# Moving the first units of cross attention into the heads of the last causal batch

## The reference

```
q = x@Wq; c = x@Wkv_down; k = c@Wk_up; v = c@Wv_up      (16 heads of 32, rotary on 24 of 32)
x = layernorm(x + causal_softmax(q k^T / sqrt(32)) v)
s = coef * (x @ W_qkv[:D].T) @ ctx^T                      (ctx: 4 x 512 x 512, keys and values)
keep the 54 largest scores of a row, softmax over them
x = layernorm(x + (att @ ctx) @ W_o.T)
x = layernorm(x + mixture of 8 gated experts(x), weights from a router)
```

## Time and profile before

| | us |
|---|---|
| median of 3 runs (1635.18 to 1636.54) | 1636.16 |
| the profiled execution | 1635.91 |
| its span, first to last instruction | 1634.1 |
| PE busy in it | 1471.2 (90%) |
| DVE busy | 1186.5 (73%) |
| ACT busy | 900.4 (55%) |
| POOL busy | 767.7 (47%) |

### The profile page before, as it was taken

The page is one execution under the profiler, slowest core; times in us unless marked ns, Lnnn a source line. Parts: engine busy times, 40 slices in busy tenths (PEclk is TensorE's granted clock), DMA queues, the critical chain, the costliest instruction groups (busy, mean ns, idle before and its releaser), DMA issues.

```text
span 1634.1 us, 27867 instructions
## 1 busy us (share of the span) xinstructions
PE 1471.2 (90%) x10404; PEld 902.3 (55%) x10404; DVE 1186.5 (73%) x2030; ACT 900.4 (55%) x1452; POOL 767.7 (47%) x693
## 2 busy tenths in 40 slices
PE   6898888988788898587999999999999999999984
PEld 3466666566544454243665666566656665666554
DVE  4767787968459999967776667666766676667657
ACT  4367575766544553555465556555655565556542
POOL 5355362712212314888474456445644564456422
PEclk9799988988599999788999999999999999999997
DMA  9500010002011110210010001000110011000002
GB/s 288 213 27 2 29 53 29 27 28 104 27 52 52 52 53 1 65 66 13 27 40 26 27 26 36 31 27 27 35 32 27 26 29 37 27 27 28 12 1 103
DMA packets 68173, 74.72 MB, mean 46 GB/s; under 512 B 9021, under 2 KB 46525, under 8 KB 67017
## 3 DMA queue, kind: packets, MB, share of 16 engines
q1 hardware_dynamic: 67464, 68.73, 13.0%
q10 hardware_dynamic: 576, 4.19, 0.7%
HBM read 49.66 MB, written 10.49 MB: 37 GB/s over the span
## 4 chain that ended last, share of the span: by engine, by line
PE 65%; DVE 13%; issue 8%; POOL 6%; ACT 4%; DVEq 0%; ACTq 0%; POOLq 0%
PE banks L1177 48%; PE banks L920 6%; PE banks L1029 2%; PE banks L1013 2%; DVE nmf L1566 2%; PE banks L974 2%; PE banks L991 1%; POOL xsum L824 1%; POOL xsum L821 1%; ACT pf L1271 1%; DVE top L1698 1%; DVE wk L1694 1%; PE banks L1015 1%; DVE attf L1705 1%; POOL xc L829 1%
## 5 line engine op out<-in xcount | busy, mean ns | idle before, releaser
L1177 PE MATMUL banks<-xc,w 128*128 128x512 f16 x2688 | 588.7, 381 | 15.8 <-ACT banks L1220 15.8
L1177 PEld LDWEIGHTS banks<-xc,w 128*128 128x128 f16 x2688 | 263.7, 98 | 335.4 <-ACT banks L1220 21.2
L1177 PE MATMUL banks<-wd,mid 128*128 128x256 f16 x2688 | 296.5, 273 | 4.7 <-ACT banks L1220 2.8
L1177 PEld LDWEIGHTS banks<-wd,mid 128*128 128x128 f16 x2688 | 262.8, 98 | 39.3 <-ACT banks L1220 3.1
L897 POOL TENSOR_TENSOR mid<-m,mid 128x512 f16<-128x512 f32 x64 | 75.0, 1172 | 315.0 <-ACT mid L1220 314.9
L1220 ACT ACTIVATE banks<-banks 128x512 f32<-128x512 f32 x192 | 108.3, 578 | 186.5 <-PE banks L1177 186.5
L897 POOL TENSOR_TENSOR mid<-msum,mid 128x512 f16<-128x512 f32 x128 | 185.8, 1470 | 1.3 <-ACT mid L1220 1.3
L1511 DVE SCALAR_TENSOR_TENSOR w<-stage,w 128x512 f16<-128x512 f32 (+1 forms) x56 | 62.2, 1150 | 104.4 <-ACT w L1220 104.4
L1220 ACT ACTIVATE mid<-msum 128x512 f16<-128x512 f32 x128 | 81.1, 634 | 85.4 <-DVE msum L1881 29.2
L795 POOL TENSOR_TENSOR plo<-pf,phi 128x1280 f16<-128x1280 f32 x24 | 63.8, 2665 | 117.1 <-ACT phi L1220 116.9
L1566 DVE TENSOR_REDUCE nmf<-banks 128x1 f32<-128x512 f32 (+3 forms) x256 | 107.2, 481 | 10.2 <-PE banks L993 9.8
(11 more groups left out here) (253 smaller groups left out, 2967.0 us busy)
## 6 DMA issues: line engine op xcount, KB each, us to landing
stage<-w_fold SPq DMA_DIRECT2D x24, 256.0 KB, 2.9
stage<-in_Wg SPq DMA_DIRECT2D x24, 256.0 KB, 3.2
stage<-in_Wu SPq DMA_DIRECT2D x24, 256.0 KB, 3.1
stage<-in_Wd SPq DMA_DIRECT2D x24, 256.0 KB, 2.8
vcat<-vnext SPq DMA_DIRECT2D x8, 528.0 KB, 3.3
x_in<-in_x SPq DMA_DIRECT2D x4, 1024.0 KB, 6.5
x_res<-in_x SPq DMA_DIRECT2D x4, 1024.0 KB, 5.8
c_raw<-in_ctx SPq DMA_DIRECT2D x4, 1024.0 KB, 5.5
```

Of the source, the lines that this page charges most:

```text
L1177: mm = nc.tensor.matmul(out, l(x, i), r(y, i), start=start and i == 0 and j == 0, stop=stop and i == k - 1 and j == 2, skip_group_check=True)
```

## The change

The units of B_FIRST are put into the lists of the last causal batch. New lists A_LAST_PE, A_LAST_ACT, A_LAST_DVE, A_LAST_POOL hold the heads' units of batch 3 and, marked `b:`, the units of cross attention; FIRST_BANK gives those other banks. The search `first.0` stands on DVE in front of comb.3, and A_FIN behind it. The wqw split moves ahead (ACT: in front of exp.10; DVE: behind mT.3). The chain that makes coef, and the split of the router's weights, go to the start of the kernel, in front of the first batch. SP loads the context of batch 0 ahead of W_q, as soon as the projections of the last batch are made, and load_x1(0) no longer waits for the last bk.

```
+A_LAST_PE = steps("""
+    bk.0 bq.5 q1.0 k1.0 bk.1 q1.1 bq.6 k1.1 q1.2 bk.2 k1.2 pv.0 bq.7 q1.3 bk.3 k1.3 mT.1 bq.8 pv.1 bk.4 bq.9 pv.2 bq.10 b:cT.0 pv.3
+    bq.11 bk.5 b:cT.1 bq.12 bk.6 mT.2 b:cT.2 pv.4 bq.13 bk.7 b:cT.3 bq.14 pv.5 bk.8 pv.6 bk.9 bq.15 pv.7 bk.10 b:wo.0 pv.8 b:wo.1 bk.11
+    b:wo.2 mT.3 pv.9 b:wo.3 bk.12 b:A.0 pv.10 bk.13 b:A.1 pv.11 bk.14 b:A.2 pv.12 b:A.3 bk.15 b:xT.0 pv.13 b:xT.1 b:sc.0 pv.14
+    b:xT.2 b:sc.1 pv.15 b:xT.3 b:sc.2 b:sc.3 b:CW.0 b:CW.1 b:CW.2 b:CW.3
+""")
+A_LAST_ACT = steps("""
...
+    b:cT.2 pv.4 hi.6 exp.7 b:cT.3 pv.5 exp.8 pv.6 hi.8 exp.9 pv.7 hi.9 wqw.0 exp.10 pv.8 hi.10 b:wo.0 exp.11 b:wo.1 pv.9 b:wo.2
+    exp.12 b:wo.3 pv.10 hi.12 exp.13 b:A.0 pv.11 hi.13 b:A.1 exp.14 b:A.2 pv.12 hi.14 exp.15 b:A.3 pv.13 b:xT.0 b:xT.1 pv.14 b:sc.0
+    b:xT.2 pv.15 b:sc.1 b:xT.3 b:sc.2 b:sc.3 b:CW.0 b:CW.1 b:first.0 b:first.1 b:CW.2 b:CW.3
+""")
+A_LAST_DVE = steps("""
...
+    max.14 comb.0 max.15 lo.8 mT.3 wqw.0 b:wo.0 b:wo.1 comb.1 b:wo.2 lo.12 b:wo.3 comb.2 lo.14 b:xT.0 b:xT.1 b:xT.2 b:xT.3 b:first.0
+    comb.3
+""")
+A_LAST_POOL = steps("""
+    lo.1 lo.2 lo.5 b:cT.0 b:cT.1 b:cT.2 b:cT.3 lo.9 lo.10 lo.13 b:A.0 b:A.1 b:A.2 b:A.3 b:CW.0 b:CW.1 b:CW.2 b:CW.3
+""")
+FIRST_BANK = {"cT": (6, 7, 6, 7),
+              "wo": (0, 1, 2, 0),
+              "A": (1, 2, 0, 1),
+              "xT": (2, 0, 2, 6),
+              "sc": (1, 0, 7, 3),
+              "CW": (4, 5, 1, 2)}
...
+            sp.wait_ge(a_ready["row"], a_upto(B - 1, ("row", 2 * TT - 1)))
+            load_context(0)
             for k in ("q1", "k1"):
...
-            load_context(0)
...
-            sp.wait_ge(st_ready, B * H + FREE)
             sp.wait_ge(bw_lo, 1)
             load_x1(0)
             sp.wait_ge(x1_written, NT)
...
+            for u in A_LAST_DVE:
+                if u == ("b:first", 0):
+                    dve.wait_ge(st_ready, B * H + FREE)
...
+            heads(A_FIN, B, None)
             for b in range(B - 1):
                 cross(B_BODY_DVE, b, b + 1)
```

More of the change, by code:

```diff
@@ L517, in wait_low, with b_bank, mixed @@
                 eng.wait_ge(p_lo_pool, b * len(LOW_POOL) + (LOW_POOL.index(i) + 1 + FREE))
-        def b_bank(u):
-            return banks[:, B_BANK[u[0]][u[1]], :]
+        def b_bank(u, own):
+            first = own == 0 and u[0] in FIRST_BANK
+            return banks[:, (FIRST_BANK if first else B_BANK)[u[0]][u[1]], :]
+        def mixed(u):
+            return (u[0][2:], u[1]) if u[0].startswith("b:") else None
         def count(b, u):
@@ L832, in _ @@
                 pool.memset(rank[:, e:e + 1], float(E - e)).then_inc(ranks, 1)
-            cross([u for u in B_FIRST if u[0] in COPIED], 0)
+            for u in A_LAST_POOL:
+                if mixed(u):
+                    cross([mixed(u)], 0)
+                else:
+                    heads([u], B - 1, None)
             cross(B_BODY_POOL, 1)
@@ L926, in _, with wait_bank @@
             pe.wait_ge(consts, 3)
+            def wait_bank(seq, n, b, nxt, earlier):
+                v, before = bank_before(LAST_BANK, seq, n, earlier)
+                if v is None:
+                    return
+                if mixed(v):
+                    pe.wait_ge(b_drained[mixed(v)[0]], upto(0, mixed(v)))
+                else:
+                    of = nxt if v[0] in A_NEXT else b
+                    pe.wait_ge(a_drained[A_KIND.get(v[0], v[0])], a_upto(of - 1 if before else of, v))
             def heads(seq, b, nxt, earlier, first=0, end=None):
@@ L935, in heads @@
                         bank, done = a_bank(u), a_ready[A_KIND.get(k, k)]
[L936 to L939, removed]
+                        wait_bank(seq, n, b, nxt, earlier)
                     if k == "xT":
@@ L1135, in cross @@
                         three(bank, lambda x, i: attT[:, t % 2, x, i, :], lambda y, i: cw[:, y, i, :], 4, b_ready[k])
-            cross(B_FIRST, None, 0, [])
-            for k in ("wo", "A", "CW", "xT", "sc"):
+            for n, u in enumerate(A_LAST_PE):
+                if mixed(u):
+                    if u == ("b:wo", 0):
+                        pe.wait_ge(max_done, B * H * 4 + FREE)
+                    if u == ("b:sc", 3):
+                        pe.wait_ge(exp_done, B * H + FREE)
+                    wait_bank(A_LAST_PE, n, B - 1, B, A_PE)
+                    cross([mixed(u)], None, 0, [])
+                else:
+                    heads(A_LAST_PE, B - 1, B, A_PE, n, n + 1)
+            for k in ("q1", "k1", "mT", "pv"):
+                pe.wait_ge(a_drained[k], a_upto(B - 1, (k, A_PER[k] - 1)))
+            for k in ("cT", "wo", "A", "CW", "xT", "sc"):
                 pe.wait_ge(b_drained[k], upto(0, (k, 3)))
@@ L1315, in _ @@
                     heads([u], None, 0)
[L1316 to L1324, removed]
             act.wait_ge(s_loaded, 96)
@@ L1330, in _ @@
             scaled(wr16[:, :, 0:E], wr_raw[:, :, :], SW).then_inc(wr_step, 1)
+            heads(own_part(A_ACT, ("res", "ln")), 0, 1)
+            with act.Fori(1, B - 1) as b:
+                heads(A_ACT, b, b + 1)
             def slice_scaled(q):
@@ L1391, in cross @@
                         act.wait_ge(att_ready, upto(own - 1, u))
+                        if own == 0 and t == 0:
+                            act.wait_ge(coef_step, COEF_STEPS)
                         act.wait_ge(b_drained["wo"], upto(0, ("wo", 3)))
[L1393 removed]
+                        nc.scalar.activation(tsc[:, t, :], b_bank(u, own), ACT.Copy, scale=coef[:, 7:8]).then_inc(b_drained[k], 1)
                     elif k in ("top", "first"):
@@ L1408, in cross @@
                         differences_high(0, t)
-            cross(B_FIRST[:4], None, 0)
+            for u in A_LAST_ACT:
+                if mixed(u):
+                    cross([mixed(u)], None, 0)
+                elif u[0] == "wqw":
+                    act.wait_ge(bq_loaded, 16)
+                    scaled(wqw[:, 0], raw_q[:, :, :], SW).then_inc(bw_hi, 1)
+                else:
+                    heads([u], B - 1, None)
             heads(A_FIN, B, None)
-            act.wait_ge(coef_step, COEF_STEPS)
-            cross(B_FIRST[4:], None, 0)
             cross(B_BODY_ACT, 0, 1)
@@ L1648, in _ @@
                     heads([u], None, 0)
[L1649 to L1661, removed]
             chain = Chain(dve, coef_step)
@@ L1676, in _ @@
             low(wr16[:, :, E:2 * E], wr_raw[:, :, :], wr16[:, :, 0:E], SW).then_inc(wr_step, 1)
+            dve.wait_ge(cat_stored, 16)
+            dve.wait_ge(fold_stored, 5 * 16)
+            heads(own_part(A_DVE, ("res", "ln")), 0, 1)
+            with dve.Fori(1, B - 1) as b:
+                heads(A_DVE, b, b + 1)
             def top_k(t0, b):
@@ L1743, in cross @@
                 assert chain is None or chain.n == B_STEPS, chain.n
-            cross(B_FIRST, None, 0)
+            for u in A_LAST_DVE:
+                if u == ("b:first", 0):
+                    dve.wait_ge(st_ready, B * H + FREE)
+                if mixed(u):
+                    cross([mixed(u)], None, 0)
+                elif u[0] == "wqw":
+                    dve.wait_ge(bw_hi, 1)
+                    low(wqw[:, 1].rearrange("p t n -> p (t n)"), raw_q[:, :, :].rearrange("p t n -> p (t n)"),
+                        wqw[:, 0].rearrange("p t n -> p (t n)"), SW).then_inc(bw_lo, 1)
+                else:
+                    heads([u], B - 1, None)
+            heads(A_FIN, B, None)
             for b in range(B - 1):
```

22 lines of the change are left out of this document (8 added, 14 removed).

## The result

The changed kernel takes 1637.13 us (median of 20 runs, 1634.53 to 1644.34) against 1633.97 for the kernel before (20 runs, 1629.55 to 1637.18): ratio 1.0024 with a 95% interval of 1.0013 to 1.0034, so 2 to 6 us slower. A later comparison of the two gave 1.0018 (1.0006 to 1.0029). Both intervals lie above 1, so the change costs time; whether it costs more or less than 0.2% they leave open.

The account below looks back on a forecast made before the run. No engine bounds the opening of cross attention; it is a chain of waits. The search starts 12.2 us earlier, but the closing norm and context load behind it put out.1 at 517.0 against 512.79: 1635.91 plus 4.2, forecast 1640, range 1632 to 1648.

Parts of the forecast that it names:

- The give-back: Behind the search: closing norm 11.3 us, then batch 1's context load 5.5, put out.1 at 517.0 instead of 512.79, +4.2.
- the rule: Body behind the first search: out.1 starts 54.5 us after the search starts, whenever that is.
- The terms taken as nothing: Coefficient chain moved to the kernel's start, context load, x1 load, CW products and search length: 0 us; coefficient chain 1.8 uncovered.
- The cT units: Four units of context transposes on PE before pv.7's end delay it by 2.8 us, bounds 0 and 4.9.
- the prediction's links: Eight successive pieces on ACT, PE and DVE from pv.7's end to the first search, summing to 55.1 us.
- link 3: New wait: ACT's wo.0 waits for DVE's wqw, exp.11 queues behind it, PE's bk.12 waits for exp.11: 5.4 us.
- link 2: PE at the lower clock: bk.11, wo.2 and mT.3's four small transposes, 3.2 us.
- links 7 and 8: PE restarted from sc.0 to xT.3, 12.0 us; then sc.1 and xT.3 on ACT, xT.3 on DVE, 1.7.
- the even point of 458.3: First search's start at which out.1 would come neither earlier nor later than in the kernel before.
- A: Rival: PE's gaps fill, upper clock holds through the last batch, search from 455.2 or 452.4, -3.1 to -5.9 us; chance 0.18.
- B: Rival: a further PE stretch before the search at 1.2 GHz, or another ACT wait; +10 to +12 us; chance 0.14.
- C: Rival: the context load behind the search does not bind, DVE does; top.2 1.6 us earlier, 1634; chance 0.16.

Follow-up runs that it names:

- exp.11 first: The changed kernel with exp.11 put ahead of wo.0 on ACT: 1636.34 us, ratio 1.0014 to the kernel before.
- the early load: The changed kernel with SP loading batch 1's context without waiting for x1_written, only the x1 load waiting: 1633.96 us, ratio 1.0003 to the kernel before.
- one swap on DVE: The changed kernel with wqw.0 ahead of mT.3 on DVE: 1633.55 us, ratio 0.9998 to the kernel before.

## Why the prediction was right

Forecast 1640, range 1632 to 1648, slower likeliest; measured 1637.13. By the ratio the change costs 3.9 us, in the second comparison 2.9; the sum said 4.2. Most of the miss in the absolute time is the start of the sum: the profile of before and its three runs lay some 2 us above the median of its 20.

**The give-back, the step that carries the sign, held.** Search end to x1_written: 11.5 us (475.0 to 486.5), predicted 11.3. From there over the load to the transposes 6.2, predicted 0.15 + 5.5. From the first transpose to A.0 8.1, where I took 8.8 from the landing. A.0 to out.1 10.8, predicted 10.85. out.1 lies 54.5 to 55.2 behind the search; the rule said 54.5. The experiments show the cause and not only the size: moving the norm alone restores 39.1, freeing the load alone takes 4.3 off, which is what the second wait left.

The load took 6.0 us, 0.5 more than in the kernel before, where no other load was on its way; here SP issues the rows of x1 0.43 us behind it. In the ten profiles in which they follow it like that the load takes 6.0 to 6.5 us; the later context loads, which go alone, take 5.4 to 5.8. The estimate of 4.4 us from the Trainium skill's page "DMA: Bandwidth & Descriptors" (Anatomy of one DMA) is again below the trace; that section is on copies issued from POOL, and this one is issued by SP.

**The terms taken as nothing held.** The chain of coef runs in the first batch now, and from the first to the second conversion of row maxima there it is 24.7 us in after and 24.8 in the kernel before. The search takes 17.8 us, as before.

**The cT units**: pv.7 starts 45.6, 48.3 and 49.1 behind the mark in before, and 50.3, 50.3, 50.3 and 53.2 in after. Means differ by 3.4; I took 2.8 within 0 to 4.9.

**The new start of the search was put too late.** From pv.7's end I summed 55.1 us; after's profile has 52.2. By the prediction's links: 1 took 5.6 (5.8), 2 took 2.4 (3.2), 3 took 5.6 (5.4), 4 took 11.7 (12.1), 5 took 10.7 (11.0), 6 took 3.9 (3.9), 7 and 8 together 12.4 (13.7). The new wait of link 3 is there, 4.93 us, in the timeline of ACT in after, but the prediction had its way to PE wrong: it led it over exp.11 to bk.12, and the run with exp.11 first shows that it goes over wo.0's bank to wo.3. The sum for the link was right (5.4, measured 5.6), its path was not. ACT:

```profile
416.77 0.60 ACT L1261 ACTIVATE woT<-banks 128x512 f16<-128x512 f32 x1 [4.93 <-DVE wqw L1551]
417.26 1.23 ACT L1312 ACTIVATE pf<-banks 128x1280 f32<-128x1280 f32 x1
```

The over-sized terms are link 2, priced at the lower clock throughout, and links 7 and 8: the loss I charged for each restart of PE was smaller: sc.0 took 4.44 us and not the 5.28 of the earlier trace rows. In three of four profiles the search therefore started 104.9 behind the mark and not 108.6; the third has 108.6 exactly.

**The test that failed.** I wrote that I was wrong in sign if the first MAX8 started before 458. It started at 457.15, and the sign held. A point counted from the span's start of one execution is no test when the mark itself moves by 4 us; counted from the mark of the first profile the even point of 458.3 is 104.4, which no profile of after went below, though three come within 0.5. Against an early execution of before (out.1 at 155.3) even that point would have been too late.

**Where luck helped.** By the prediction's own rule a search 104.9 behind the mark costs 0.5 us against the first profile of before, and out.1 did come 0.5 us later there (159.4 against 158.9), not 4.2. That the timed runs still lie 3 us apart comes from two things that the sum did not hold: the kernel before often runs faster than the execution that I started from, and the changed kernel has late executions of its own (out.1 at 163.8). The sign and the mechanism were predicted; that the size fits so well is in part two errors that cancel, a search put 3.7 us too late and a start taken 1.9 us too high.

**The rivals.** A was right in its mechanism: the clock of the last batch did rise to 0.85, as "TensorE: Matmul & The Clock Gate" (Part 1) of the Trainium skill would have it, and the search gained more than I summed. It wasn't enough, since 16.6 us were owed. B, a whole link (4, 5 or 7) at the lower clock, shows in no profile. After's third profile has a lower clock (0.79 in 357 to 437) and out.1 4.4 us late, but 2.9 of these are there at pv.7 already (53.2 behind the mark against 50.3), ahead of the links. C fell with the early load.

## What to carry to other kernels

Ask of every unit that is moved ahead of another what stood there and who waits for it: here a norm of 11 us that cost nothing in an idle stretch was pushed behind the search, and a load through one semaphore hung on it. The gain of the early start was real and could be kept by moving the displaced work too; with that, and one swap on DVE, the same idea is 0.8% faster instead of 0.2% slower. Compare stretches from a mark inside the trace, and over several executions, before you read 2 us out of two profiles.

## What was not expected of the hardware

Four normed rows on DVE take 1.92 us alone and 3.59 beside POOL's low parts of cxT, which cost the early load 1.7 us of its gain, and 3.59 again beside the low parts of CW with the norm ahead of the search. In both runs a row that starts while POOL's instruction is under way takes 1.37 to 1.38 us, the others 0.54.

In one execution a wait cost more than its length. With the 4.9 us wait for wqw, PE's granted clock in the 10 us around it was 0.57; without it 0.98. In that execution exp.12 came 4.8 us earlier, counted from DVE's last conversion of row maxima, and the search a further 2.1. The timed runs gain 3 to 5 us by the same swap, so they do not show the excess.

Executions of one and the same kernel differ by 4 us in the time of the mark, though the batches ahead of it do the same work, and by 4.5 us in the stretch behind it. Which of them a profile catches decides more than the change did. Part of it is there before the first batch: DVE's first conversion of row maxima starts at 82.0 to 82.6 us in ten of the profiles and at 85.1 to 86.2 in four. In the second profile of after (86.2) PE's granted clock was 0.83 from 40 to 60 us, in the first (82.2) it was 1.00. All four late ones are of the changed kernel or its variants, but the first instruction that the change moved there runs only at 74.6 us, behind the delay. What starts an execution on one or the other course the runs do not show, and it stays open; so does the question whether a part of the 3 us lies there.
